# Two of the 32 row-maximum chunks of each group of the first attention copied by ScalarE, folded by GpSimd and ended by VectorE

## What is computed

```python
scores = jnp.einsum('bhqd,bhkd->bhqk', q, k) * scale
probs = jax.nn.softmax(scores, axis=-1)
ctx = jnp.einsum('bhqk,bhkd->bhqd', probs, v)
```

## Time and profile before

| | before |
|---|---|
| median of 3 runs | 1661.97 us |
| profiled execution | 1661.77 us |
| span of its trace | 1659.8 us |
| PE busy (matmuls) | 1609.1 us, 97% |
| DVE busy | 1491.0 us, 90% |
| ACT busy | 1281.8 us, 77% |
| POOL busy | 266.8 us, 16% |
| mean granted TensorE clock | 0.991 |

### The profile page before, as it was taken

How to read it: one execution, slowest core, us unless ns; L and a number is a source line. 1 busy time by engine, 2 the same in 40 slices (tenths; PEclk the granted TensorE clock), 3 DMA queues, 4 the chain that set the end, 5 groups by cost and what they waited for, 6 DMA issues and landing times.

```text
span 1659.8 us, 39596 instructions
## 1 busy us (share of the span) xinstructions
PE 1609.1 (97%) x14128; PEld 636.9 (38%) x14128; DVE 1491.0 (90%) x2168; ACT 1281.8 (77%) x2424; POOL 266.8 (16%) x623
## 2 busy tenths in 40 slices
PE   6899999999999999999988999999999999999999
PEld 3322222222222223787653222222222222237877
DVE  6999999999999997787678999999999999937765
ACT  3399999999999998433224999999999999983321
POOL 1410000000000000000012222333332233320000
PEclk9989999999999999999998999999999999999999
DMA  6943344334354321200404232222222322112000
GB/s 160 296 98 70 63 76 84 63 64 84 69 139 87 73 60 44 64 1 0 117 15 132 59 66 57 51 51 65 57 55 62 62 57 51 55 49 58 14 13 26
DMA packets 72126, 114.70 MB, mean 69 GB/s; under 512 B 12464, under 2 KB 27824, under 8 KB 71984
## 3 DMA queue, kind: packets, MB, share of 16 engines
q1 hardware_dynamic: 71984, 112.63, 29.2%
HBM read 71.96 MB, written 40.63 MB: 68 GB/s over the span
## 4 chain that ended last, share of the span: by engine, by line
PE 54%; DVE 35%; issue 7%; ACT 1%; DMA 1%; SPq 0%; DVEq 0%; POOLq 0%; ACTq 0%
DVE mneg L1306 28%; PE psum L785 18%; PE psum L767 11%; PE psum L737 7%; PE psum L887 5%; PE psum L843 5%; PE psum L848 2%; PE psum L700 2%; PE psum L823 2%; PE psum L720 1%; PE psum L682 1%; DVE area L1356 1%; DVE area L1390 1%; DVE stats L1199 1%; DVE area L1340 1%
## 5 line engine op out<-in xcount | busy, mean ns | idle before, releaser
L1055 ACT ACTIVATE area<-psum 128x512 f32<-128x512 f32 x2048 | 1097.2, 600 | 42.1 <-PE psum L767 13.7
L785 PE MATMUL psum<-area 128*32 128x256 f32 x8192 | 655.2, 392 | 0.4 <-POOL area L1568 0.4
L767 PE MATMUL psum<-area 51*128 51x512 bf16 x2048 | 639.2, 385 | 2.5 <-DVE vsb_b L1256 1.4
L1312 DVE CUSTOM_DVE_ANT_0 xn<-psum,band 128x1024 f32<-128x1024 f32 x512 | 588.4, 1220 | 10.3 <-PE psum L737 9.3
L1306 DVE TENSOR_REDUCE mneg<-psum 128x1 f32<-128x1024 f32 x512 | 581.0, 1211 | 7.0 <-PE psum L737 6.9
L785 PEld LDWEIGHTS psum<-area 128*32 128x32 f32 x8192 | 162.1, 108 | 400.7 <-issue 259.1
L737 PE MATMUL psum<-area 48*128 48x512 bf16 x1024 | 301.6, 385 | 8.2 <-DVE mneg L1306 5.1
L767 PEld LDWEIGHTS psum<-area 51*128 51x128 bf16 x2048 | 141.0, 94 | 427.0 <-ACT area L1055 353.3
L737 PE MATMUL psum<-k_max_b,area 48*128 48x512 bf16 x1024 | 292.8, 385 | 5.4 <-DVE mneg L1312 4.7
L1549 POOL TENSOR_TENSOR mparts<-mneg,nought 128x16 bf16<-128x16 f32 x64 | 14.1, 221 | 742.3 <-DVE mneg L1306 501.1
L1100 ACT ACTIVATE area<-psum 128x512 f32<-128x512 f32 x64 | 38.2, 599 | 115.9 <-PE psum L848 115.8
(11 more groups left out here) (89 smaller groups left out, 1092.1 us busy)
## 6 DMA issues: line engine op xcount, KB each, us to landing
ctx_rows<-area SPq DMA_DIRECT2D x64, 256.0 KB, 2.1
area<-q_stacks SPq DMA_DIRECT2D x32, 384.0 KB, 6.8
area<-k_stacks SPq DMA_DIRECT2D x64, 192.0 KB, 5.6
area<-q_stacks_b SPq DMA_DIRECT2D x32, 384.0 KB, 5.3
area<-q_stacks SPq DMA_DIRECT2D x32, 192.0 KB, 4.6
area<-q_stacks_b SPq DMA_DIRECT2D x32, 192.0 KB, 3.4
area<-ctx_rows SPq DMA_DIRECT2D x16, 256.0 KB, 4.1
area<-inv_rows SPq DMA_DIRECT2D x16, 256.0 KB, 4.5
```

The costliest lines, as they stand in the source:

```text
L767: pe.matmul(psum[:, BANK_OF["exp", g, u, head], :], k_st[lo:lo + ROWS + PARTS, buf, 0 if a else head // 2, kt * P:(kt + 1) * P], q_st[lo:l ...
L785: mm = pe.matmul(psum[head * VW:(head + 1) * VW, BANK_OF["ctx", g, qh], cols], vaug[:, buf, kt, head, :], probs[:, u % PRING, head, cols], ...
L1055: act.activation(probs[:, u % PRING, head, :], psum[:, BANK_OF["exp", like, u, head], :], ACT.Exp, scale=SCALE).then_inc(bank_freed, 1)
L1312: dve.tensor_tensor_reduce(band_out[:, c % 2, :], slot, band[:, at:at + SEQ], 1.0, -3.0e38, ALU.add, ALU.max, mneg[:, qh, col:col + 1]).th ...
```

## The change

In groups 1 to 15 of attention 0, chunks 4 and 20 are no longer reduced by VectorE. ScalarE copies such a chunk's 1024 columns out of PSUM (`hold_scores`) behind the second exponential of unit 5 or 13. GpSimd folds the copy from 1024 columns to 128 in three rounds (`narrow_down`): far - near, the maximum of that with zero, and near added; each waits for the one before. VectorE takes the maximum of the 128 columns (`end_maximum`) behind chunk 10 or 26. TensorE's instructions and their order stay; its wait for the bank pair of a held chunk is now on the ScalarE copy, and its other chunk waits are on the maxima counter counted in the new order.

```diff
+ON_ACT = (4, 20)
+ENDED_BEHIND = {10: 4, 26: 20}
@@ max_scores
-                if not isinstance(g, int) or n >= 2:
-                    pe.wait_ge(max_used, n if in_feed(a, g, c) else n - 1)
+                if in_feed(a, g, c):
+                    pe.wait_ge(max_used, n)
+                elif n >= 2:
+                    G, old = divmod(n - 2, CHUNKS)
+                    if is_held(*divmod(G, GROUPS), old):
+                        pe.wait_ge(held, held_before(G, old) + 1)
+                    else:
+                        pe.wait_ge(max_used, maximum_at(*divmod(G, GROUPS), old) + 1)
@@ scalar
+            def hold_scores(g, c):
+
+                k = held_before(g, c)
+                act.wait_ge(max_ready, CHUNKS * g + c + 1)
+                if not isinstance(g, int) or k:
+                    act.wait_ge(narrowed, k)
+                bank = max_bank(0, g, c)
+                act.copy(hold[:], psum[:, bank:bank + 2, :].rearrange("p b c -> p (b c)")).then_inc(held, 1)
@@ exps
+                    c = LEAD + 2 * u + head // 2 - CHUNKS
+                    if a == 0 and ahead and head % 2 and c in ON_ACT:
+                        hold_scores(g + 1, c)
@@ split_dense_weights
+                dve.wait_ge(narrowed, len(ON_ACT) * (GROUPS - 1))
@@ vector
+            def end_maximum(g, c):
+
+                qh, head, qt = chunk_of(c)
+                col = (head % 2) * (CPH // 2) + (head // 2) * (BT // HALF) + qt
+                dve.wait_ge(narrowed, held_before(g, c) + 1)
+                dve.tensor_reduce(mneg[:, qh, col:col + 1], narrow[:], AX.X, ALU.max, negate=True
+                                  ).then_inc(max_used, 1)
+
             def group(a, g):
                 for c in range(CHUNKS):
-                    maxima(a, g + 1, c)
+                    if not is_held(a, g + 1, c):
+                        maxima(a, g + 1, c)
+                    if a == 0 and c in ENDED_BEHIND:
+                        end_maximum(g + 1, ENDED_BEHIND[c])
@@ gpsimd
+            def narrow_down(g, c):
+
+                k = held_before(g, c)
+                pool.wait_ge(held, k + 1)
+                n = SEQ // 2
+                for i in range(3):
+                    near, far = hold[:, 0:n], hold[:, n:2 * n]
+                    s0 = 3 * k + i + 1
+                    pool.tensor_tensor(far, far, near, ALU.subtract).then_inc(held_less, 1)
+                    pool.wait_ge(held_less, s0)
+                    pool.sem_inc(above_started, 1)
+                    pool.tensor_scalar(far, far, 0.0, None, ALU.max).then_inc(held_above, 1)
+                    pool.wait_ge(held_above, s0)
+                    if i < 2:
+                        pool.tensor_tensor(near, near, far, ALU.add).then_inc(held_halved, 1)
+                        pool.wait_ge(held_halved, 2 * k + i + 1)
+                        n //= 2
...
+                pool.tensor_tensor(narrow[:], near, far, ALU.add).then_inc(narrowed, 1)
@@ group
+                    for step in range(2):
+                        c = LEAD + 2 * u + step - CHUNKS
+                        if a == 0 and ahead and c in ON_ACT:
+                            narrow_down(g + 1, c)
```

More of the change, by code:

```diff
@@ L79, in chunk_of, with is_held, maximum_at, held_before @@
     return qh, head, qt
+ON_ACT = (4, 20)
+ENDED_BEHIND = {10: 4, 26: 20}
+STEPS = []
+for _c in range(CHUNKS):
+    STEPS += ([] if _c in ON_ACT else [_c]) + ([ENDED_BEHIND[_c]] if _c in ENDED_BEHIND else [])
+NARROW = 128
+def is_held(a, g, c):
+    return a == 0 and c in ON_ACT and not (isinstance(g, int) and g == 0)
+def maximum_at(a, g, c):
+    return CHUNKS * (GROUPS * a + g) + (c if a or isinstance(g, int) and g == 0 else STEPS.index(c))
+def held_before(g, c):
+    return len(ON_ACT) * (g - 1) + ON_ACT.index(c)
 EVENTS = GH * UNITS + 2 * HALF
@@ L194, in hybrid_kernel @@
         wkv_b = [sb(f"wkv_b{i}", [P, DK, KV_HEADS * HD]) for i in range(2)]
+        wu_at = nc.sbuf_base
         wu_hi = sb("wu_hi", [P, DK, INNER // P, P], F32R)
@@ L211, in hybrid_kernel @@
         mT = sb("mT", [CPH * PARTS, HALF, P], BF16)
+        narrow = sb("narrow", [P, NARROW])
         sums_at = nc.sbuf_base
@@ L276, in hybrid_kernel, with over @@
                  + [parts_mid[:, i] for i in range(2)] + [parts_top[:, 0], parts_far[:, 0]])
-        def over(name, at, shape):
-            return nc.alloc_sbuf_tensor_at(name, shape, F32R, offset=at)
+        def over(name, at, shape, dt=F32R):
+            return nc.alloc_sbuf_tensor_at(name, shape, dt, offset=at)
         wg_hi = over("wg_hi", vsb_at, [P, DK, INNER // P, P])
@@ L289, in hybrid_kernel @@
         xd_lo = [over(f"xd_lo{c}", at, [P, DK, BANK]) for c, (_, at) in enumerate(xd_at)]
+        hold = over("hold", wu_at, [P, SEQ], F32)
         w_raw = [xnT[:, 2 * i:2 * i + 2].rearrange("p c k t -> p (c k t)").rearrange("p (k n) -> p k n", k=DK)
@@ L332, in hybrid_kernel @@
         mask_started, max_started = sem("mask_started"), sem("max_started")
+        above_started = sem("above_started")
+        held, held_less, held_above, held_halved, narrowed = (
+            sem(s) for s in ("held", "held_less", "held_above", "held_halved", "narrowed"))
         x_biased, x_attended, x_fed = sem("x_biased"), sem("x_attended"), sem("x_fed")
@@ L1308, in maxima @@
                     if not isinstance(g, int) or c >= 2 or g:
-                        dve.wait_ge(max_used, CHUNKS * G + c - 1)
+                        dve.wait_ge(max_used, maximum_at(a, g, c) - 1)
                     dve.sem_inc(max_started, 1)
@@ L1559, in split_max @@
                 pool.tensor_tensor(mparts[:, qh, :, 2, :], view(mres2), view(nought), ALU.add).then_inc(mparts_ready, 1)
+            def narrow_down(g, c):
[14 more added lines that the diff above has]
+                        n //= 2
+                if not isinstance(g, int) or k:
+                    first = c == ON_ACT[0]
+                    old = ON_ACT[ON_ACT.index(c) - 1]
+                    pool.wait_ge(max_used, CHUNKS * (g - first) + STEPS.index(old) + 1)
+                pool.tensor_tensor(narrow[:], near, far, ALU.add).then_inc(narrowed, 1)
             def mask_probs(a, g, u, ahead):
```

## The result

The changed kernel took 1805.07 us in the median (1804.29 to 1806.0), against 1661.63 for the kernel before: ratio 1.0862, 95% interval 1.0843 to 1.0881. Slower, as forecast, but by 143 us and not by 22: far outside the range.

The account below looks back on a forecast made before the run. VectorE was taken as the bound at 18.09 us a half, TensorE just behind; 17.99 + 0.08 + 0.48 + 0.20 + 0.10 = 18.85 us, + 0.76 over 30 halves, rounded to + 22 us, gave 1684 us, range 1670 to 1712.

Parts of the forecast that it names:

- The bound and the floor behind it: Attention 0: VectorE bounds at 18.09 us a half, TensorE needs 17.99, so VectorE's relief brings at most 0.10 a half.
- TensorE has room: Rival, 6%: TensorE's 1.11 us step is set by hand-overs, ScalarE sets the pace, 13 us faster: 1649 us.
- The copy's stall: ScalarE's 1.04 us copy delays an exponential, so TensorE's second score matmul of unit 6 waits 0.48 us, once a half.
- The sum without the fold's share: Half a group: TensorE's pace 17.99, context copy 0.08, stall from ScalarE's copy 0.48 us; leaves out 0.20 and 0.10.
- VectorE's end: VectorE's 128-column reduction that ends a held chunk's maximum: taken at 0.20 us, bounds 0.15 and 0.30.
- The fold's length: GpSimd's three rounds from 1024 to 128 columns: 6.5 to 6.9 us, taken as 6.7, one-input operations priced from selects.
- covered up to 6.5 us: A GpSimd fold up to about 6.5 us costs nothing behind chunk 10; each further 0.1 us costs 0.1 a half.
- my own line: Whole kernel's time against GpSimd's fold length: 1684 us at 6.7 us, each further us costing 30 us.
- the fold is late: Rival, 22%: GpSimd's operations or gaps are longer than the rows'; 1702 us at a 7.3 us fold, 1723 at 8.
- The range: Whole kernel: 1670 to 1712 us, leaving out the fast rivals, the null case and a fold beyond 7.6 us.

Follow-up runs that it names:

- e2: Changed kernel without ScalarE's copy and GpSimd's fold; chunks 4 and 20 are made but unread, VectorE's end reduces a constant: 1662.57 us, ratio 0.9999.
- e1: Changed kernel with VectorE's end of the held maxima behind chunks 13 and 29 instead of 10 and 26: 1674.09 us, ratio 1.0075.
- e3: Changed kernel without GpSimd's fold, keeping ScalarE's copy and TensorE's wait for it; VectorE's end reduces a constant: 1673.86 us, ratio 1.0066.
- e6: Changed kernel, end still behind chunks 10 and 26, with the three maxima with zero left out of GpSimd's fold: 1674.06 us, ratio 1.0074.
- e5: Changed kernel with VectorE's end of the held maxima behind chunks 11 and 27, one chunk later: 1711.55 us, ratio 1.0299.
- e4: Changed kernel with ten repeated score matmuls on TensorE in front of chunks 12 and 28 of attention 0: 1750.08 us, ratio 1.0525.

## Why the prediction was wrong, point by point

- **The bound and the floor behind it: right.** VectorE was the bound by a hair, TensorE stood less than 0.1 us a half behind. e2 gives 18.13 us a half against 18.07 and no gain; no step that makes a chunk is under 1.10 (the shorter ones, 0.89 to 1.08, stand behind the last chunk, as before the change). "TensorE has room" is out, and with it every version that only takes work off VectorE with TensorE's order as it is.
- **The copy's stall: right.** 0.46 against 0.48, copy 1.02 against 1.04. The sum without the fold's share, 17.99 + 0.08 + 0.48 = 18.55, is met by e1, e3 and e6 at 18.56; that it is met so closely is in part luck, since e2's floor is 0.06 above the forecast and the copy adds 0.43 to it, 0.05 less. The half copy removes the stall as the same reckoning says. This stall alone makes the kernel slower (e3), so the direction of the forecast came true for a reason that it gave.
- **VectorE's end: right in size.** Its record is 0.28 us, and it takes 0.20 of VectorE's time (308.42 - 308.22), as forecast.
- **The fold's length: the step that failed.** I took 6.7 us, with 6.9 as the top of the sum; it is 8.83. Of the 2.13 too few, (1.48 - 0.64) + (0.84 - 0.43) + (0.52 - 0.32) = 1.45 are the maxima with zero, whose price I took from the selects; 0.48 are the longer gaps, where I had priced the extra semaphore instructions at nothing; 0.20 is having taken the middle of the two-input bounds. The rule "covered up to 6.5 us" was right: e6's fold of 5.39 us is covered, and the change pays 20.90 - 18.56 = 2.34 us a half in waits, which is 8.83 - 6.49. So was its slope: e5, with one more chunk of cover, pays 19.77 - 18.56 = 1.21. With 8.83 us in it, my own line (1684 at 6.7 us, 30 us for each us more) gives 1684 + 2.13 x 30 = 1748, near e4's 1750, of which 4 to 5 are its matmuls in group 0.
- **The clock: missing from the sum, the second step that failed.** I priced a stall of TensorE at its own length and the clock behind it at nothing. Behind the gap of 2.3 us the granted clock falls to its lower level for the next steps in 24 of 29 halves, 55 to 59 us in all. No stall in my forecast was over 0.5 us, so the mis-sized fold brought in a mechanism that the forecast never met. The rival "the fold is late" named the right mechanism with 22%, but its line of 30 us per us ends at 1723 for 8 us, and lacks the clock as well.
- **The range.** Its top took the fold at 7.6 us. A form that no row showed (a tensor-scalar in float32 on GpSimd) had been bounded by another form of operation alone, and the bound from the other side, the two-input operation of the same width, would have given 1.27 for 0.64 and a fold of about 8 us at the top. The measured 1.48 lies above both, and the clock would still have been missing.

The Trainium skill, GPSIMD Engine Reference, Elementwise, gives about 1.8 cycles an element as the best case of a loop (768 ns for 512 elements at 1.2 GHz) and about 2.6 for the two-input `tensor_tensor`. The trace agrees with the second: 2.13 ns a column, 2.6 such cycles. The maximum with zero, one input, is far from the best case: 2.50 ns a column, 3.0 cycles, and 1.48 us for 512, more than the two-input one beside it (1.27).

## What to carry to other kernels

Relief of the bounding engine is worth the distance to the next one, so measure that first: here TensorE's own step pace in a stretch where nobody held it up said 0.1 us a half before the change was made. Work that is handed through three engines is free only while each hand-over is ahead of its reader; give the last reader more distance than the sum needs (three chunks here cost nothing and were worth 131 us). And a long stall of TensorE has to be priced twice, once as idle time and once as the clock behind it: the gap of 2.3 us here cost both, the one of 1.2 us only the first.

## What the runs showed of the hardware

- A GpSimd tensor-scalar (maximum with a constant) in float32 takes 1.48, 0.84 and 0.52 us for 512, 256 and 128 columns, 2.5 ns a column, slower than the two-input add or subtract beside it (1.27, 0.73, 0.45: 2.1 ns a column) and 2.3 times the select's 0.635 at 512.
- Behind a gap of 2.3 us between TensorE's starts (1.94 idle) the granted clock fell to 0.50 in 24 of 29 halves and stayed there for up to about five steps, a different number from half to half (22.3, 23.7, 25.3 us against 20.90); behind one of 1.2 us (0.82 idle) it stayed at 1.00 in all 29. Ten needless matmuls in place of the idle time kept it up and made the kernel 55 us faster.
- A ScalarE copy of 1024 columns from PSUM takes 1.02 us, and one of 512 takes 0.59. The long one, put between exponentials, stalls TensorE by 0.46 us; the short one does not.
